# Four batches through token mixing into attention: a new order at the hand-over, and two subtractions given to GpSimd

## The reference

```python
def _L0_tok_ref(x, d_gamma, Wq, bq, Wk, bk, Wv, bv, Wo, bo, prelu_a):   # per batch, T = 1024, 64 wide
    q, k, v = x @ Wq + bq, x @ Wk + bk, x @ Wv + bv
    scores = jnp.einsum('btd,bsd->bts', q, k)
    retained = jnp.einsum('bts,bsd->btd', d_gamma * scores, v)
    y = retained @ Wo + bo
    return jnp.where(y >= 0, y, prelu_a * y)

def _L0_attn_ref(x, qkv_w, qkv_b, proj_w, proj_b, rpb_table):           # 8 heads of 8
    qkv = (x @ qkv_w + qkv_b).reshape(Bw, Nw, 3, nh, dh)
    attn = jnp.einsum('bnhd,bmhd->bhnm', q * dh ** -0.5, k) + bias
    return softmax(attn) @ v -> (Bw, Nw, Cd) @ proj_w + proj_b

h = _L0_tok_ref(x, ...)
h = h + _L0_attn_ref(_layernorm(h), ...)
h = h + _L0_ffn_ref(_layernorm(h), ...)          # top 2 of 8 experts, gelu, 64 -> 128 -> 64
```

## Time and profile before

| | |
|---|---|
| runs | 560.37, 564.43, 560.65 us, median 560.65 us |
| profiled execution | 558.65 us, its span from first to last instruction 556.9 us |
| busy share of the span | PE 93%, DVE 82%, ACT 64%, POOL 14% |
| costliest lines | L869 DVE row maxima 301.6 us; L724 ACT exponentials 278.1 us; L1400 PE values 164.1 us |
| granted PE clock | mean 0.974 of full |
| token stage, hand-over, attention, experts | to about 100, 132, 465 and 557 us |

### The profile page before, as it was taken

One profiled execution on the slowest core, in us unless ns is written; L12 is line 12 of the kernel. 1 busy time (PEld: TensorE's weight loads), 2 busy tenths in 40 slices (PEclk: granted clock), 3 DMA queues, 4 the chain that ended last, 5 costly groups with the idle time before them and its releaser, 6 DMA issues.

```text
span 556.9 us, 12956 instructions
## 1 busy us (share of the span) xinstructions
PE 515.6 (93%) x4238; PEld 176.7 (32%) x4238; DVE 458.4 (82%) x540; ACT 353.8 (64%) x625; POOL 80.0 (14%) x180
## 2 busy tenths in 40 slices
PE   7999898557999999999999999999999888999996
PEld 6233332221333333333333333333333343233221
DVE  2668687778999999999999999999999786766644
ACT  2011222323889889898898898988988766445442
POOL 9601010203010010100100101001000451111000
PEclk9999999865999999999999999999999999999999
DMA  7910369373233232232332322323234101000000
GB/s 267 237 33 2 89 197 258 86 212 97 56 88 80 58 93 76 74 82 65 86 80 60 87 74 82 78 61 89 77 96 113 53 11 32 22 9 12 19 20 19
DMA packets 51095, 46.33 MB, mean 83 GB/s; under 512 B 26265, under 2 KB 39034, under 8 KB 51066
## 3 DMA queue, kind: packets, MB, share of 16 engines
q1 hardware_dynamic: 51066, 45.94, 30.5%
HBM read 29.75 MB, written 16.17 MB: 82 GB/s over the span
## 4 chain that ended last, share of the span: by engine, by line
PE 67%; DVE 5%; issue 1%; DMA 1%; ACT 1%; SPq 1%; POOL 0%; DVEq 0%; ACTq 0%; POOLq 0%
PE ps L1400 24%; PE ps L1312 13%; PE ps L1385 13%; PE ps L1533 5%; PE ps L1559 5%; DVE nmax L869 2%; PE ps L1326 1%; PE ps L1389 1%; DVE probs L1144 1%; PE ps L1546 1%; SPq L408 1%; PE ps L1450 1%; DMA maxima<-max_t 1%; PE ps L1556 1%; PE ps L1437 0%
## 5 line engine op out<-in xcount | busy, mean ns | idle before, releaser
L869 DVE TENSOR_REDUCE nmax<-ps 128x1 f32<-128x1024 f32 x256 | 301.6, 1218 | 18.7 <-PE ps L1312 9.9
L724 ACT ACTIVATE probs<-ps 128x512 f32<-128x512 f32 x512 | 278.1, 596 | 56.0 <-PE ps L1385 46.0
L1400 PE MATMUL ps<-probs,v_ring 128*32 128x256 f32 x2048 | 164.1, 393 | 0.0
L1312 PE MATMUL ps<-k_ring,q_ring 48*128 48x512 bf16 x512 | 102.9, 399 | 6.9 <-DVE nmax L869 6.9
L1385 PE MATMUL ps<-q_ring,k_ring 51*128 51x512 bf16 x512 | 101.3, 384 | 5.9 <-DMA q_ring<-maxima 1.7
L1312 PEld LDWEIGHTS ps<-k_ring,q_ring 48*128 48x128 bf16 x512 | 24.8, 93 | 113.7 <-issue 98.8
L1400 PEld LDWEIGHTS ps<-probs,v_ring 128*32 128x32 f32 x2048 | 40.5, 108 | 61.7 <-issue 36.8
L1144 DVE TENSOR_TENSOR probs<-probs,ps 128x1024 f32<-128x1024 f32 x32 | 39.0, 1220 | 25.4 <-PE ps L1546 20.1
L743 ACT ACTIVATE probs<-ps,wide_w 128x1024 f32<-128x1024 f32 x32 | 35.3, 1114 | 35.0 <-PE ps L1533 33.2
L890 DVE SCALAR_TENSOR_TENSOR gated<-ps,v_s,gamma_sb 128x1024 f32<-128x1024 f32 x32 | 40.7, 1280 | 10.9 <-PE ps L1234 10.7
L577 POOL TENSOR_TENSOR max_p<-nmax,zeros 128x8 bf16<-128x8 f32 x32 | 6.5, 202 | 282.4 <-DVE nmax L869 259.3
(11 more groups left out here) (162 smaller groups left out, 327.6 us busy)
## 6 DMA issues: line engine op xcount, KB each, us to landing
k_ring<-qk_parts SPq DMA_DIRECT2D x64, 96.0 KB, 2.4
q_ring<-qk_parts SPq DMA_DIRECT2D x64, 96.0 KB, 2.4
gamma_sb<-gamma_t SPq DMA_DIRECT2D x4, 1024.0 KB, 10.2
v_padded<-v_pad SPq DMA_DIRECT2D x4, 1024.0 KB, 5.0
v_ring<-v_padded SPq DMA_DIRECT2D x32, 128.0 KB, 3.2
outputs<-o_t SPq DMA_DIRECT2D x32, 128.0 KB
qk_parts<-qk_h SPq DMA_DIRECT2D x8, 384.0 KB, 4.3
x_ring<-bias_parts SPq DMA_DIRECT2D x32, 96.0 KB, 3.1
```

Of the source, the lines that this page charges most:

```text
L724: A.activation(probs[:, s % 4, HALF * j:HALF * (j + 1)], ps[:, key_bank(s, j), :], ACT.Exp).then_inc(exp_done[j], 1)
L869: V.tensor_reduce(nmax[:, par, s:s + 1], ps[:, bank:bank + 2, :].rearrange("p a n -> p (a n)"), AX, ALU.max, negate=True).then_inc(s1_redu ...
L1312: return mm(ps[:, bank + j, :], q_ring[rows, u, P * s:P * (s + 1)], k_ring[rows, u, HALF * j:HALF * (j + 1)], start=True, stop=(s > 0 or j ...
L1400: last = mm(ps[VC * j:VC * (j + 1), PVB, 0:2 * P], v_ring[:, u, m, :], probs[:, m % 4, 2 * P * j:2 * P * (j + 1)], start=(m == 0), stop=(m ...
```

## The change

Four things move, and two instructions change engines.

- DVE in batches 2 and 3: `rest_part` of batch `b - 2` stands behind the gate of tile 3 instead of tile 2, and `low_part` behind `norm_var` at tile 6 instead of behind the gate of tile 3. At a batch's last tile `norm_scale` comes before `leave_v`. In the last batch the first row maximum of head 0 is taken before that `norm_scale`.
- PE: the first score tile of head 0 is computed at tile 6 of batch 3; further on, the score tiles stand in other places between the projections.
- DVE in the hand-over: `norm_var`, `rest_part`, `norm_scale` and the maxima are in a new order, and both `low_part` are gone from it.
- POOL: it makes the low parts of the last two batches, behind its four `power` and ahead of `split_maxima` of head 0, with the same waits that DVE had.
- SP: in the last batch v and the low parts are stored after the maxima of head 0 have been sent to DRAM and before they are fetched from there, instead of behind both.

```diff
--- before.py
+++ after.py
@@ -421,13 +421,18 @@
                 store_parts(0, qk_h)
                 sp.wait_ge(qk_m_ready, b + 1)
                 store_parts(1, qk_m)
+
+                def store_rest():
+                    sp.wait_ge(v_pad_ready, b + 1)
+                    sp.dma_start(v_scratch[NH * b:NH * b + NH, :, :].rearrange("h p n -> p h n"),
+                                 v_pad[:, :, :, :].rearrange("p h m c -> p h (m c)")).then_inc(v_stored, 16)
+                    sp.wait_ge(qk_l_ready, b + 1)
+                    store_parts(2, qk_l)
+
                 if b == B - 1:
-                    send_max_rows(0, 0, 0, lambda: None)
-                sp.wait_ge(v_pad_ready, b + 1)
-                sp.dma_start(v_scratch[NH * b:NH * b + NH, :, :].rearrange("h p n -> p h n"),
-                             v_pad[:, :, :, :].rearrange("p h m c -> p h (m c)")).then_inc(v_stored, 16)
-                sp.wait_ge(qk_l_ready, b + 1)
-                store_parts(2, qk_l)
+                    send_max_rows(0, 0, 0, store_rest)
+                else:
+                    store_rest()
                 if b == 0:
                     for i in range(PARTS):
                         sp.wait_ge(qk_stored[i], 2 * 16)
@@ -550,6 +555,12 @@
 
             for n in range(B):
                 power(n)
+
+            for n in range(B - 2, B):
+                pool.wait_ge(qk_r_ready, n + 1)
+                pool.wait_ge(qk_m_ready, n + 1)
+                pool.wait_ge(qk_stored[2], n * 2 * 16)
+                gp.tensor_tensor(qk_l[:, :], qk_rest[:, :], qk_m[:, :], ALU.subtract).then_inc(qk_l_ready, 1)
 
             def bias_residual(b):
                 h_b = h_all[:, NT * b:NT * (b + 1), :]
@@ -949,39 +960,41 @@
                         bias_low()
                     if b == 1 and s in (1, 2):
                         b2_parts(s - 1)
-                    if b >= 2 and s == 2:
+                    if b >= 2 and s == 3:
                         rest_part(b - 2)
-                    if b >= 2 and s == 3:
-                        low_part(b - 2)
                     if b >= 1 and s == 4:
                         activate(b - 1)
                     if b >= 1 and s == 5:
                         first_center(b - 1)
                     if b >= 1 and s == 6:
                         norm_var(b - 1)
+                    if b >= 2 and s == 6:
+                        low_part(b - 2)
+                    if b == B - 1 and s == NT - 1:
+                        row_max(0, 0, 0)
+                    if b >= 1 and s == NT - 1:
+                        norm_scale(b - 1)
                     if b + 1 < B and s == NT - 1:
                         leave_v(b + 1)
-                    if b >= 1 and s == NT - 1:
-                        norm_scale(b - 1)
 
             def first_maxima(a, z):
                 for i in range(a, z):
                     row_max(i // NT, i % NT, i // NT)
 
-            first_maxima(0, 2)
             activate(B - 1)
             first_center(B - 1)
+            first_maxima(1, 2)
+            norm_var(B - 1)
             rest_part(B - 2)
-            norm_var(B - 1)
+            first_maxima(2, 3)
             norm_scale(B - 1)
-            first_maxima(2, 3)
-            low_part(B - 2)
             first_maxima(3, 4)
+            first_maxima(4, 5)
             rest_part(B - 1)
-            first_maxima(4, 8)
+            first_maxima(5, 6)
+            first_maxima(6, 9)
             turn_maxima(0, 0, None)
-            low_part(B - 1)
-            first_maxima(8, 2 * NT)
+            first_maxima(9, 2 * NT)
 
 
             def invert_sums(b):
@@ -1326,6 +1339,17 @@
                         last = mm(ps[:, bank + 1, HALF - P:HALF], flip_b[:, :], x_ring[:, u, i, :],
                                   start=False, stop=(i == PARTS - 1))
                 last.then_inc(s1_ready, 1)
+
+            def first_scores(a, z):
+                for i in range(a, z):
+                    if i == 0:
+                        pe.wait_ge(consts_ready, 1)
+                    if i < 2:
+                        pe.wait_ge(tok_gated, B * NT - 1 + i)
+                    if i % NT == 0:
+                        pe.wait_ge(operands[i // NT], 16 * N_OPERANDS)
+                    scores_upper(i // NT, i % NT, i // NT)
+                    scores_lower(i // NT, i % NT, i // NT)
 
             for at in range(2):
                 score(at)
@@ -1351,32 +1375,23 @@
                         turn_bias()
                     if b == 0 and s == 7:
                         spread_bias()
-
-            def first_scores(a, z):
-                for i in range(a, z):
-                    if i == 0:
-                        pe.wait_ge(consts_ready, 1)
-                        pe.wait_ge(tok_gated, B * NT)
-                    if i % NT == 0:
-                        pe.wait_ge(operands[i // NT], 16 * N_OPERANDS)
-                    scores_upper(i // NT, i % NT, i // NT)
-                    scores_lower(i // NT, i % NT, i // NT)
-
-            first_scores(0, 2)
+                    if b == B - 1 and s == 6:
+                        first_scores(0, 1)
+
+            first_scores(1, 2)
             turn_y(B - 1)
             turn_hn(B - 2)
             project_qk(B - 2)
             first_scores(2, 4)
             project_vv(B - 2)
+            first_scores(4, 5)
             turn_hn(B - 1)
-            first_scores(4, 5)
             project_qk(B - 1)
-            first_scores(5, 6)
+            first_scores(5, 7)
             project_vv(B - 1)
-            first_scores(6, 2 * NT)
+            first_scores(7, 2 * NT)
             pe.wait_ge(qk_r_ready, B)
             pe.wait_ge(v_pad_ready, B)
-
 
             def scores_by_key(s, u, j):
```

## The result

The changed kernel takes 557.3 us (median of 20 runs, 554.9 to 564.2), the kernel before 564.2 us beside it on the same chip (20 runs, 558.7 to 569.7). The ratio is 0.991, 95% interval 0.988 to 0.994; it is taken over the fast executions alone, so it differs from the quotient of the two medians, 0.988. The forecast was a ratio of 0.989 (554.6 against 560.65) and, with 0.52, a gain of over 1%; 0.9% counts as within 1%. The profiled execution took 554.93 us (before 558.65, forecast 552.65).

A forecast was written before the change was run, and what follows sets the result against it. The prediction took DVE's back-to-back row maxima, with PE waiting, to end the path to attention; 3.4 + 0.4 + 2.9 less 0.7 made 6.0 us, so 554.6 us against a 560.65 median, 8-in-10 range 551.4 to 557.8.

The forecast's parts named there:

- Token stage: DVE's work in batches 2 and 3: reordering brings the last gate to 94.5 instead of 97.9 us, 3.4 us gained.
- a last gate not 3 us earlier: End of the token stage: the forecast counts as wrong if the last gate is not 3 us earlier.
- `low_part` is only moved; it costs what it cost: DVE, batch 2: the moved instruction was charged no extra time in the 1.55 us gain.
- the two terms it is part of: Token stage: 0.56 us from batch 2's earlier first gate, 1.55 us from batch 2's rest_part to the next first gate.
- To the second `rest_part`: Hand-over from the last gate: 0.4 us lost, then 0.8 gained, net 0.4; second rest_part at about 112.5 us.
- From there to the last score: Hand-over from the second rest_part: a maximum, the low part and a POOL wait leave DVE's path, net 2.9 us gained.
- The collision with `norm_scale`: Hand-over: DVE first by 0.15 us, so no cost; rival with POOL first loses 1.7 us, 556.3, chance 0.10.
- The fetch: SP's fetch of maxima behind the stores: lands at about 125.8 us, 0.7 us after PE could use it.
- The sum: Whole kernel: 6.7 less 0.7 gives 6.0 us gained, profiled 558.65 to 552.65; forecast 554.6 us, chance 0.48.
- is gained for the whole kernel: Path to attention's first matmul: any gain there carries to the end, since attention and experts run behind in series.
- my fourth rival: Hand-over: the freed time is not on the path through the second rest_part, little more than token stage stays; 557.3, chance 0.07.

The follow-up runs named there:

- experiment 1: Kernel before with only the token-stage moves of rest_part, low_part, norm_scale and leave_v: 561.1 us, ratio 0.995.
- Experiment 5: Changed kernel with low_part ahead of norm_var at tile 6 of batches 2 and 3: 558.7 us, ratio 0.988.
- experiment 3: Changed kernel with the two hand-over low parts back on DVE: 559.4 us, ratio 0.990.
- experiment 6: Changed kernel with extra matmuls on constants (fillers), whose result nobody reads, in PE's hand-over waits: 552.7 us, ratio 0.979.
- experiment 7: Changed kernel with the edits of experiment 4, Experiment 5 and experiment 6 together: 553.3 us, ratio 0.983.
- experiment 8: Kernel of experiment 7 with POOL's split of head 0's maxima ahead of its second low part: 553.2 us, ratio 0.981.
- experiment 2: Kernel before with the two hand-over low parts made on POOL and every order kept: 566.0 us, ratio 1.004.
- experiment 4: Changed kernel with SP's old order, the maxima fetched before v and the low parts are stored: 557.3 us, ratio 0.986.
- experiment 10: Kernel of experiment 8 with one filler behind each first score from the eighth tile on, instead of two behind head 1's: 554.3 us, ratio 0.984.
- e11: Kernel of experiment 9 without the three fillers ahead of batch 3's project_qk, and one instead of two behind scores from the seventh tile: 565.7 us, ratio 1.002.
- experiment 9: Kernel before, with no part of the change, plus the fillers of experiment 6 at the same hand-over places: 561.9 us, ratio 0.999.

## Why the forecast was right in its mechanism and too large by its sum

- **Token stage, forecast 3.4 us, measured 2.55: this term was mis-sized.** By the prediction's own sign of being wrong, a last gate not 3 us earlier, the forecast failed here. One step that failed is "`low_part` is only moved; it costs what it cost". It costs DVE the same, but it was moved beside POOL's power and lengthens that from 1.64 to 2.58 us, in experiment 1 too. In batch 2 `norm_scale` starts some 0.4 us later for it (75.50 against an estimated 75.1); in batch 3 it comes later than the last gate and the power costs nothing there. The other step is `norm_scale` ahead of `leave_v`: the two terms it is part of, forecast 0.56 and 1.55, measured 0.40 and 0.91. `leave_v`, now directly ahead of the gate that needs it, takes 0.82 us up to the next start instead of 0.62, so 0.2 us are lost at the start of batch 2 and again of batch 3. Together that is 0.8 of the 0.85 us. Experiment 5 brings back 0.67 us, but by both of its effects. I had weighed the shared interface for the instructions that change engines, not for one that only changes neighbours.
- **To the second `rest_part`: right.** 17.98 us from the last gate, as forecast, with 3.46 us of idle time; that the low part taken from DVE here is worth nothing is shown by experiment 3.
- **From there to the last score: right.** 12.18 us against 12.3. POOL's low part took 2.12 us (2.49 beside `norm_scale`), I had taken 2.4. One thing came out right by luck: the second one did not begin when ACT was done (forecast 114.95, in the trace 115.68) but at 116.43, when the store of batch 2's low part had freed the buffer, a wait that I had left out. At half clock the split lost 0.1 us by it, at full clock 2.3 (experiments 6 to 8).
- **The collision with `norm_scale`: right.** DVE was first, by 0.18 us, and took 0.68. By the Trainium skill's rule alone ("GPSIMD Engine Reference", Key points), that a DVE instruction with two SBUF inputs collides with GpSimd, it would have been charged; the trace agrees that they collide, but which of them pays goes by the start (experiment 2: DVE 2.60 us).
- **The fetch, forecast 0.7 us, measured 0.4.** The wait exists, with the data there 3.07 us after the issue, and experiment 4 takes it away. That the fetch stood behind the stores agrees with the ring order of the Trainium skill ("DMA: Bandwidth & Descriptors", Queues, rings and completion order).
- **The sum and what becomes of it.** At attention's first matmul 5.6 us, forecast 6.0. The sentence that carried it to the end, that what is gained there "is gained for the whole kernel", did not hold in this pair of executions. It put the clock behind that point at nothing: half clock was to end at about 132 and ended at 135.2. The first rounds took 0.9 us of the gain (5.62 to 4.73), the way to 424 us 0.15, the stretch at 430 to 440 us 0.8. With the 0.4 missing at attention's start (0.85 in the token stage, less 0.1 in the hand-over and 0.3 at the fetch) that is how 552.65 became 554.93.
- **Did the earlier arrival cost the extra round? Not shown, and experiment 2 speaks against it.** In the seven traces without fillers full clock comes back some time after attention begins, however early that is:

| kernel | first attention matmul, us | full clock from, us | between, us |
|---|---|---|---|
| before | 131.84 | 138.7 | 6.9 |
| e1 | 130.03 | 138.4 | 8.4 |
| e2 | 133.07 | 142.2 | 9.1 |
| e3 | 128.97 | 137.6 | 8.7 |
| e4 | 127.92 | 141.2 | 13.2 |
| e5 | 126.79 | 135.8 | 9.0 |
| after | 126.26 | 135.2 | 8.9 |

The latest start (e2) has as long a stretch at half clock as the earliest (after). The profile before, from which I forecast, has the shortest of all. So the 0.9 us is more likely a difference between two executions than a price of the change. Experiments 8 and 10 show what rounds at half clock cost, not that an early start brings them.
- **Open.** Stretches of lower clock behind 430 us appear in some traces, of both orders of the hand-over (440 to 460 us in e1, 450 to 500 in e11), and not in others, and I can't say that the change causes or lengthens them. At about equal clock (0.968 after, 0.965 and 0.974 before) the medians are 555.5 against 562.8 and 560.8 us, 7.3 and 5.3 apart. How much of the gain survives on average is known only to the interval of the ratio, 3.3 to 6.7 us, which holds the forecast of 6.0.
- **A coincidence.** The median after, 557.3 us, is the figure of my fourth rival ("little more than the token stage stays"). Attention started 5.6 us sooner and the token stage alone gave a ratio of 0.995 (experiment 1), so the rival did not hold. Its figure was counted from a median of 560.65 us; that of 20 runs is 564.2.
- **The chances.** With a forecast 0.4 us from the limit, 0.52 for "faster by over 1%" was nearly a coin toss; a share for a worse clock than in the profile before, which was one of the best, would have put the larger part within 1%.

## What to carry to other kernels

A moved instruction costs what it cost only if its new neighbours on other engines don't mind: list for each what runs on GpSimd at that moment, and who starts first. A profile is one execution: where the clock differs between executions, price the rounds behind a changed stage at both clocks before carrying a gain to the end, and look at several traces before calling a loss a price of the change. Fillers hurt ahead of anything that others wait for (experiment 9), and with too few of them PE stayed at half clock in attention's first rounds (10 and 11). An instruction given to an idle engine brings its buffer's wait with it, so it belongs behind the work on the path (here the split).

## What the runs showed of the hardware

- Where DVE and GpSimd collided here, the one that started second took longer, by a little less than what was left of the first: GpSimd's power of 128x8 took 2.58 instead of 1.64 us beside a DVE subtraction of 1.22 us begun 0.14 us earlier; DVE's 128x512 multiplication 2.60 instead of 0.69 us, begun 0.07 us behind GpSimd's 2.12 us.
- GpSimd's subtraction of 128x1024 float32 to bf16 takes 2.12 us alone, 1.75 times DVE's 1.21.
- A higher mean clock is no gain by itself: experiment 9 had 0.986 to 0.989 in executions of 559.8 to 561.2 us, the kernel before 0.974 in executions of 558.8 to 561.4. The matmuls that raised it had put off attention's start by 2.4 us.
